# First attention heads in pairs: two transposed heads per evacuation, key products ahead of the weighted values, one reciprocal for two heads, bias sums in another order

## What is computed

```python
x = x + L0_xattn(layernorm(x), ctx, ctx)        # 16 heads of 16, biases, probabilities clipped from below at 1e-12
x = x + L0_ffn(layernorm(x))                    # weights and activations quantized to fp4 blocks of 16
x = x + L1_xattn(layernorm(x), ctx, ctx, mask)  # 16 heads of 64, masked
x = x + L1_ffn(layernorm(x))                    # fixed point, piecewise linear gelu
```

```python
scores = q @ k.T / sqrt(16); scores -= max(scores)
attn = clip(softmax(scores), 1e-12, None); attn /= sum(attn)
ctx = attn @ v                                   # all heads side by side, then @ Wo.T + bo
```

## Time and profile before

| | |
|---|---|
| median of 3 runs | 1078.9 us (1078.84 to 1080.39) |
| the profiled execution's own time | 1078.07 us |
| its span in the trace | 1076.2 us |
| busy in the span | PE 932.8 us (87%), DVE 751.2 (70%), ACT 612.5 (57%), POOL 146.9 (14%) |
| span of a crossing pass's heads, with the steps around them | 70 us of 312 to 382 |

### The profile page before, as it was taken

The page is one execution under the profiler, slowest core; times in us unless marked ns, Lnnn a source line. Parts: engine busy times, 40 slices in busy tenths (PEclk is TensorE's granted clock), DMA queues, the critical chain, the costliest instruction groups (busy, mean ns, idle before and its releaser), DMA issues.

```text
span 1076.2 us, 17112 instructions
## 1 busy us (share of the span) xinstructions
PE 932.8 (87%) x5092; PEld 585.8 (54%) x5092; DVE 751.2 (70%) x2390; ACT 612.5 (57%) x1693; POOL 146.9 (14%) x209
## 2 busy tenths in 40 slices
PE   3387998999978889999988888899997899989985
PEld 1244565456555546455755555555755555645653
DVE  3989796464698789266397878556469869836448
ACT  1268532794559722498277942289356963269642
POOL 2422200133000000034000000023300000013200
PEclk7689999999999999999999999999999999999999
DMA  9400000000000000000000010000000000000000
GB/s 289 153 1 2 1 25 20 2 2 1 1 1 11 11 27 1 20 2 2 0 1 5 16 27 2 20 1 2 1 1 1 16 5 1 1 1 1 1 0 20
DMA packets 15331, 18.71 MB, mean 17 GB/s; under 512 B 3584, under 2 KB 12416, under 8 KB 15232
## 3 DMA queue, kind: packets, MB, share of 16 engines
q1 hardware_dynamic: 13168, 15.80, 4.6%
q10 hardware_dynamic: 2064, 1.71, 0.6%
HBM read 15.41 MB, written 2.10 MB: 16 GB/s over the span
## 4 chain that ended last, share of the span: by engine, by line
issue 57%; DVE 17%; PE 14%; POOL 6%; ACT 3%; DMA 1%; ACTq 1%; POOLq 0%; DVEq 0%
PE bank L1034 7%; POOL ring L433 3%; DVE ring L936 2%; PE bank L1312 2%; PE bank L1049 2%; POOL rstd L421 1%; DVE ring L947 1%; ACT ring L523 1%; DMA bq_s<-bq 1%; PE bank L1117 1%; PE bank L1138 1%; POOL maskbias L425 1%; DVE ring L852 1%; DVE big_k L852 1%; PE bank L1231 1%
## 5 line engine op out<-in xcount | busy, mean ns | idle before, releaser
L936 DVE CUSTOM_DVE_ANT_0 ring<-bank,maskbias 128x256 f32<-128x256 f32 x256 | 93.5, 420 | 109.0 <-issue 109.0
L523 ACT ACTIVATE ring<-bank 128x512 f32<-128x512 f32 x256 | 143.8, 590 | 39.2 <-PE bank L1049 38.6
L1049 PE MATMUL bank<-ident_s,ring 128*128 128x128 f32 x896 | 129.6, 281 | 16.8 <-ACT ring L523 8.8
L1049 PEld LDWEIGHTS bank<-ident_s,ring 128*128 128x128 f32 x896 | 98.8, 142 | 72.6 <-issue 41.8
L614 ACT ACTIVATE ring<-ring,row_max 128x256 f32<-128x256 f32 x256 | 127.2, 498 | 8.8 <-DVE row_max L936 3.6
L1034 PE MATMUL bank<-ctxT_s,wk_s 128*128 128x512 f32 x160 | 85.2, 659 | 29.0 <-DVE v L835 16.1
L421 POOL TENSOR_TENSOR rstd<-var_eps,minus_half 128x2 f32<-128x2 f32 x32 | 24.2, 761 | 612.1 <-DVE var_eps L766 612.1
L579 ACT ACTIVATE ring<-bank,row_max 128x256 f32<-128x256 f32 x192 | 88.3, 498 | 29.9 <-DVE row_max L844 29.9
L433 POOL TENSOR_TENSOR ring<-ring,row_inv 128x256 f32<-128x256 f32 x128 | 75.9, 614 | 204.9 <-DVE row_inv L943 204.9
L844 DVE TENSOR_REDUCE row_max<-bank 128x2 f32<-128x512 f32 x128 | 79.4, 682 | 13.6 <-PE bank L1117 13.5
L1034 PE MATMUL bank<-wgu_s,act_s 128*128 128x352 f32 x256 | 80.5, 468 | 3.0 <-ACT act_s L517 3.0
(11 more groups left out here) (155 smaller groups left out, 1659.2 us busy)
## 6 DMA issues: line engine op xcount, KB each, us to landing
ctxT_s<-ctxT SPq DMA_DIRECT2D x4, 512.0 KB, 3.7
x_s<-x SPq DMA_DIRECT2D x4, 512.0 KB, 3.7
w_s<-w SPq DMA_DIRECT2D x2, 1024.0 KB, 16.2
out<-act_s SPq DMA_DIRECT2D x16, 128.0 KB, 1.7
wk_s<-wk SPq DMA_DIRECT2D x1, 1024.0 KB, 11.5
wv_s<-wv SPq DMA_DIRECT2D x1, 1024.0 KB, 13.6
wq_s<-wq SPq DMA_DIRECT2D x1, 1024.0 KB, 15.7
wo_s<-wo SPq DMA_DIRECT2D x1, 1024.0 KB, 18.0
```

Of the source, the lines that this page charges most:

```text
L523: act.activation(probsT[u % TRING][:, :, :].rearrange("p a q -> p (a q)"), psum(at, key)[:], ACT.Copy).then_inc(drain(at, key), 1)
L936: ins = dve.tensor_tensor_reduce(probs[i % PRING][:, a, :], psum(at, ("s1", i))[:, a * SEQ:(a + 1) * SEQ], maskbias[:, 2 * b + a, :], -1.0 ...
L1049: ins = pe.transpose(psum(at, key)[:, c * SEQ + a * P:c * SEQ + (a + 1) * P], tile[:, a, c * P:(c + 1) * P], ident_s[:])
```

## The change

- **Two heads at once.** The transposes of two neighbouring units go into banks 4 and 5 as one job (`two_banks`, 16 jobs instead of 32, all counted on bank 4). They signal once, after the second unit, and ACT copies both with one 128x1024 instruction. The next pair's transposes wait for that one copy.
- **Keys ahead.** On PE the key chunk comes before the weighted values of the round.
- **Reciprocals by two.** DVE waits for both units' exponentials, takes one reciprocal of four sums, and then does the four multiply-and-clip steps. In the opening pass the fp4 pieces stand after the pair, no longer between its units.
- **Bias sums.** They are done in the order of tiles 3, 0, 1 (banks 7, 4, 5), then the first pair of heads, then tile 2 (bank 6). Before the first key chunk PE waits for bank 7 and for tile 1.

```diff
-        jobs.add(("t0", i), 4 + i % 2)
+    for n in range(UNITS // 2):
+        jobs.add(("t0", n), 4)
...
+        two_banks = ctx.enter_context(nc.psum_tensor("two_banks", [P, 2, 512], F32))
+        bank[4:4] = [two_banks[:, 0, :], two_banks[:, 1, :]]
...
+            def evacuate_two_probsT(at, n):
+
+                key, to = ("t0", n), PRING + 2 * n % TRING
+                act.wait_ge(*is_filled(at, key))
+                act.activation(ring[:, to:to + 2, :], two_banks[:], ACT.Copy).then_inc(drain(at, key), 1)
...
                 def normalize(u):
-                    dve.wait_ge(*is_drained(at, ("s0", u)))
-                    dve.reciprocal(row_inv[:, u, :], row_sum[:, u, :]).then_inc(inv0, 1)
+                    for i in (u, u + 1):
+                        dve.wait_ge(*is_drained(at, ("s0", i)))
+                    dve.reciprocal(row_inv[:, u:u + 2, :], row_sum[:, u:u + 2, :]).then_inc(inv0, 1)
...
+                    before_heads((3, 0, 1))
                     for i in round_units0(r):
-                        normalize(i)
+                        if i % 2 == 0:
+                            normalize(i)
+                            before_heads((2,) if i == 0 else ())
...
+            def layer0_transposes(at, group, n):
+
+                key = ("t0", n)
+                wait_free(at, key)
+                for j in range(2):
+                    u = 2 * n + j
                     pe.wait_ge(clipped0, group * UNITS + u + 1)
-                    transpose_probs(at, ("t0", u), probs0[u % PRING0])
+                    for a in range(2):
+                        for c in range(2):
+                            ins = pe.transpose(two_banks[:, j, c * SEQ + a * P:c * SEQ + (a + 1) * P],
+                                               probs0[u % PRING0][:, a, c * P:(c + 1) * P], ident_s[:])
+                ins.then_inc(fill(at, key), 1)
...
                 for r in range(1, ROUNDS0 + 2):
+                    if r <= ROUNDS0:
+                        layer1_key(at, r - 1)
                     if r >= 2:
                         layer0_weighted(at, r - 2)
                     if r <= ROUNDS0:
-                        layer1_key(at, r - 1)
-                        first = 4 * (r - 1)
-                        layer0_transposes(at, group, (first, first + 1))
+                        layer0_transposes(at, group, 2 * (r - 1))
```

More of the change, by code:

```diff
@@ L244, in sem @@
             return ctx.enter_context(nc.semaphore(name))
-        bank = [ctx.enter_context(nc.psum_tensor(f"bank{b}", [P, 512], F32)) for b in range(8)]
+        bank = [ctx.enter_context(nc.psum_tensor(f"bank{b}", [P, 512], F32)) for b in range(8) if b not in (4, 5)]
+        two_banks = ctx.enter_context(nc.psum_tensor("two_banks", [P, 2, 512], F32))
+        bank[4:4] = [two_banks[:, 0, :], two_banks[:, 1, :]]
         wq0_s, wk0_s = sb("wq0_s", [P, KC, HEADS * DK0]), sb("wk0_s", [P, KC, HEADS * DK0])
@@ L589, in layer0_heads @@
                     if r >= 1:
-                        first = 4 * (r - 1)
-                        for i in (first, first + 1):
-                            evacuate_probsT(at, 0, i)
+                        evacuate_two_probsT(at, 2 * (r - 1))
                         layer1_key(at, r - 1)
@@ L595, in layer0_heads @@
                             weighted((r - 3) // 2)
-                        for i in (first + 2, first + 3):
-                            evacuate_probsT(at, 0, i)
+                        evacuate_two_probsT(at, 2 * (r - 1) + 1)
                         if with_weights and r >= WEIGHTS_FROM:
@@ L816, in gelu, with output_bias @@
                         dve.tensor_scalar(yT[:, u, :], prev[:, 1, :], FIX, FIX, ALU.add, ALU.subtract).then_inc(y_ready, 1)
-            def output_bias(at):
-                for t in range(TILES):
+            def output_bias(at, tiles):
+                for t in tiles:
                     dve.wait_ge(*is_filled(at, ("o2", t)))
@@ L866, in layer0_heads, with before_heads @@
                         row_maxima(i)
[L867 to L871, removed]
-                            output_bias(at)
+                    if r == 0 and g is None:
+                        dve.wait_ge(values_loaded, 16 * 2)
+                    def before_heads(tiles):
+                        if r == 0 and g is None:
+                            layer0_values(at, tiles)
+                        if r == 0 and g is not None:
+                            output_bias(at, tiles)
+                    before_heads((3, 0, 1))
                     for i in round_units0(r):
-                        normalize(i)
+                        if i % 2 == 0:
+                            normalize(i)
+                            before_heads((2,) if i == 0 else ())
                         if g is None:
@@ L1132, in layer0_weighted @@
                     wait_free(at, key)
-                for u in round_units0(r):
-                    pe.wait_ge(*is_drained(at, ("t0", u)))
+                for n in (2 * r, 2 * r + 1):
+                    pe.wait_ge(*is_drained(at, ("t0", n)))
                 for c in range(2):
@@ L1188, in layer0_heads @@
                             spread_sums(at, [0])
-                        layer0_transposes(at, group, (first + 2, first + 3))
+                        layer0_transposes(at, group, 2 * (r - 1) + 1)
                         if with_weights and r >= WEIGHTS_FROM:
```

35 lines of the change are left out of this document (18 added, 17 removed).

## The result

The changed kernel takes 1090.6 us (median of 6 runs, 1089.5 to 1092.7); the kernel before took 1079.0 beside it (6 runs, 1077.9 to 1080.4). The ratio is 1.0108, with a 95% interval from 1.0095 to 1.0121: 11.6 us slower. The prediction said 1093.7.

The account below looks back on a forecast made before the run. It took a loop of waits, no full engine, to bound the heads, lengthened from 6.79 to 7.35 us a crossing round. Adding 12.3 (crossing) and 2.5 (opening) to 1078.07 gave 1092.9, as median 1093.7 us; range 1084 to 1101.

Parts of the forecast that it names:

- 1, reciprocal: Crossing round: the reciprocal starts only when both units' sums are there, 1.97 us after the first exponential.
- 2, first clip: Crossing round: first multiply-and-clip 0.20 us after the reciprocal starts; four take 1.15, the second unit clipped at 3.32.
- 3, first copy: Crossing round: after 0.11 us to PE and 0.69 for four transposes, ACT starts copying at 4.12.
- 4, second pair: Crossing round: the second pair's transposes wait for the 1.02 us wide copy plus 0.13 to PE, starting at 5.27.
- 5, second copy: Crossing round: both units must be transposed before this copy, +0.48 + 0.69 us, so it starts at 6.44.
- 6, next exponential: Crossing round: the wide copy holds ACT 0.91 us until the next exponentials, making a round 7.35 us against 6.79.
- The faster rival: Crossing rounds: the 0.95 us wait goes and nothing replaces it; 1067 us in all, chance 0.12.
- The wait is worth little: PE's 0.95 us wait before the weighted values: removing it gains at most 0.18 us a round, 1.3 a pass.
- Bias sums: nothing: Start of a crossing pass: one sum fewer saves about 0.33 us, gone at the second pair; 0.05 a pass, counted nothing.
- The opening: +2.5: Opening pass heads: +2.5 us taken between bounds of -1 and +5, with rounds of 8.1 us.
- These cost nothing: Layer 1 on PE: one value more computed a round costs nothing, as loop and last pass both took 49.3 us.
- The sum: Whole kernel: 12.3 us in three crossing passes plus 2.5 in the opening, 14.8 us slower.

Follow-up runs that it names:

- x2: The changed kernel with a bank, a count and a 512-column copy for each unit again; 1078.6 us, ratio 0.9998.
- x4: The kernel before with only the joint wide copy of two heads, weighted values still ahead of the key chunk; 1091.4 us, ratio 1.0117.
- x5: The changed kernel with each 1024-column copy made two of 512, the joint counts kept; 1093.8 us, ratio 1.0145.
- x1: The kernel before with only the key chunks moved ahead of the weighted values; 1075.3 us, ratio 0.9969.
- x6: The changed kernel copying only the first 256 of each head's 512 columns, so half the weighted sums' input is left out; 1074.0 us, ratio 0.9964.
- x3: The changed kernel with one reciprocal and two clips a unit again, wide copies and keys ahead kept; 1084.1 us, ratio 1.0050.
- x8: The kernel before plus, in crossing passes, keys ahead and new sum order; in the opening, all four sums first and paired reciprocals; 1070.9 us, ratio 0.9940.
- x7: The changed kernel with all four bias sums of the opening pass ahead of its first reciprocals; 1089.5 us, ratio 1.0106.
- x12: x8 with the third of four spread products behind the crossing heads in bank 4 instead of bank 2; 1070.5 us, ratio 0.9914.
- x9: x8 with the last unit's first-head transposes in bank 4 instead of 5 in crossing passes, making the banks' counts unequal; 1071.8 us, ratio 0.9933.

## Why the prediction was right, and where it was not

Its loop is the measured one: the first copy and the second pair wait for two heads at once. Counted from the first exponential, predicted and measured (341.33 and on):

| step | predicted | measured |
|---|---|---|
| 1, reciprocal | 1.97 | 2.03 |
| 2, first clip | 2.17 | 2.24 |
| 3, first copy | 4.12 | 4.13 |
| 4, second pair | 5.27 | 5.29 |
| 5, second copy | 6.44 | 6.41 |
| 6, next exponential | 7.35 | 7.33 |

- *Two heads at once.* Shown from three sides: x2 (undone, 6.77), x4 (alone, 7.25 from 6.79), x5 (joint counts with narrow copies, 7.45). Of the 0.69 us between x1's round and the changed kernel's, 0.38 is the joint copy and 0.31 the paired reciprocal that can only come with both units' sums (0.56 and 0.13 if the reciprocals are put first). The faster rival needed the copy at 0.74 us; it measured 1.02. x6, at 0.60, turned the sign, with 6.72 against 6.79; at 0.74 it wouldn't have: the first copy gives no more than 0.18 before the scores decide, so 6.72 + 0.14 = 6.86 (an estimate from x6's round). Within a pass the first round became 0.30 longer for the 0.42 worked out, the six others 0.54 each for 0.56, and the end 0.52 for 0.35.
- *The wait is worth little.* 0.18 a round at most was worked out; x1 has 0.15. That keys ahead gives nothing beside the longer loop was too strong: beside single reciprocals it gives 0.23 (x4, x3). Beside paired ones it wasn't tried.
- *Bias sums: nothing.* Against the kernel before, the second pair starts 0.08 earlier in the first round (6.93 against 7.01 us behind the first exponential); 0.05 was worked out. But the order isn't worthless there: with the joint copy and the old order (x4) it is 7.18, so the order gives 0.26 a pass with the joint copy (9.23 to 8.97 a first round, x4 and x3) as without (x1 and x8). And it comes with the clock: with the old order four of nine first rounds met the lower clock, at 1.4 to 1.7 us each; with the new one none of 33. That was in no term.
- *The opening: +2.5 was mis-sized*, +4.2 measured. It wasn't added up but taken between two bounds. From the second round's first exponential to the last round's it is nearly right: six rounds were 0.5 us longer in all (8.87 against 8.78 each), and the 8.1 us a round holds in rounds 2, 4 and 7 (8.13, 8.01, 8.01). What was missing lies at both ends: the first round is 2.1 longer, of which 1.25 is that TensorE's first key chunk needs all four sums and the fourth was put behind two units' clips (x7); and from the last round's first exponential to the output it is 1.6 longer (12.02 against 10.42) where a crossing pass has 0.5; that was not taken apart. Rounds 5 and 6 are long, 9.75 and 10.55. Most of it is not the clock: x5 has 9.82 and 9.92 there at full clock. The second pair's clips, which the loop waits for, run beside GpSimd. The prediction had "half a us of clips that meet POOL", in its upper bound; the rows of round 5 have 3.36 - 1.14 = 2.2:

```profile
91.06 1.00 POOL L451 TENSOR_TENSOR big_v<-big_v 128x384 f32<-128x384 f32 x1 [4.78 <-DVE big_v L760]
91.10 3.36 DVE L861 TENSOR_SCALAR ring<-ring,row_inv 128x256 f32<-128x256 f32 x4
...
93.43 0.63 PE L1147 MATMUL two_banks<-ident_s,ring 128*128 128x128 f32 x4 [1.24 <-DVE ring L861]
```

  About 0.7 us more in round 6 (x5's 9.92 less the 0.1 by which its other rounds are longer, against 10.55) is the granted clock (1.00 from 92.2 to 95.2 us, 0.50 from 95.4 to 102.1), which fell behind these waits for the clips and ahead of PE's wait for bank 7. The windows of rounds 4 and 6, and the key chunk of round 6:

```profile
78.89:86.90 8.01, 6.61 (x56) 3.96 (x56) 6.06 (x19) 6.85 (x25) 2.19 (x3) 1.00 0.01 2
...
96.65:107.21 10.56, 9.16 (x56) 4.64 (x56) 9.20 (x19) 6.86 (x26) 2.83 (x3) 0.74 0.01 2
```
```profile
96.86 3.78 PE L1050 MATMUL bank<-ctxT_s,wk_s 128*128 128x512 f32 x4 [1.09 <-ACT wgu_s L514]
```

  The same four matmuls take 3.78 us there and 1.88 in the crossing passes.
- *The extra REGISTER_ALU rows: "These cost nothing"* is the step that failed outright. They don't cost; they gain, since each takes a wait off a matmul. That loop pass and last pass were equal, 49.3 us, was read rightly before the change, but both carried two waits there; after it the loop passes have 48.9. Of the 2.5 us outside the heads 1.9 lies between the opening and the third crossing pass, and 1.1 of that is layer 1's heads (0.38 in each of three passes); the rest of it wasn't taken apart. The other 0.6 lies ahead of the first exponential and behind the third crossing pass, where executions differ by more than that.
- *The sum.* 14.8 us was forecast for the heads and 14.7 came, by two errors that cancel, which is luck: 10.5 in the crossing passes for 12.3 (1.7 of it the clock of one round of before) and 4.2 in the opening for 2.5. The 2.5 that came back elsewhere make the difference to 12.2. The rule of the Trainium skill that the prediction names ("Perfetto Trace Analysis", Optimizing Scalar/DVE Operations), on engines that are not saturated but make others wait, foretold the direction; x2 and the changed kernel, 12 us apart, agree with it. x5 adds that breaking up the instruction was not enough: with two copies under one count the kernel was slower still (1093.8). The formula of "ScalarE: Activation LUTs", What ACT_TABLE_LOAD costs, of the Trainium skill gives an estimate of 1.04 and 0.95 for the wide copy; 1.02 and 0.92 were measured.

## What to carry to other kernels

Evacuating two results as one saves per-instruction time (0.05 us here) and costs latency on both sides: the copy waits for the later one to be filled, the next producer for both to be drained. If they are single-buffered and the copying engine is not full, follow one round from a point to its like and add both waits. A wait that is visible on one engine is worth only what the next loop leaves: compute that loop before removing it. And measure the parts one by one, and each place apart: here one lost 12 us and hid others that gain 7 (x8), of which the pairs of reciprocals gain in the opening and lose in the crossing passes.

## What was not expected of the hardware

- A matmul that waits for two semaphores starts later than one whose first wait was taken by an instruction before it: 0.41 against 0.32 us behind the same exponentials (x8, x12), 0.28 against 0.20 behind a copy. The queue instructions in the traces, which the views leave out, show where this goes. In x8 the semaphore that comes last is waited for by an instruction of its own (EVENT_SEMAPHORE, at 337.11), and the weight load, which holds the other wait, starts at 337.19, 0.11 us behind the end of the exponentials' last row (337.07). In x12 the weight load itself waits for it and starts 0.05 behind (338.33 and 338.28).
- Beside three GpSimd rows (91.06 to 94.05 us in the changed kernel) VectorE's four clips took 3.36 us; the first pair's four of the same round, with GpSimd idle, took 1.14. It is so in rounds 5 and 6 of the opening of every kernel here with paired reciprocals.
- The granted clock fell behind waits of PE of 1 to 2 us in some passes and not in others of the same code. With PE's wait of 1.96 us for the sums (before, x1, x4) four of nine first rounds of a crossing pass had it (10.36 against 8.67 in before); with 1.70 us (all others) none of 33. The opening heads of x8 and x9, the same code, are 3 us apart. What decides it stays open.
